# A two-layer mixture-of-experts kernel on one core: tokens of a sample group split one slot sooner, and a shorter, earlier table of groups

## What is computed

```python
gate_scores = softmax(gate_logits)                  # one row of 4 experts per sample
topk_w, topk_i = top_k(gate_scores, 2)              # normalised to sum 1
for e in range(4):
    h = gelu(x @ ew1[e] + eb1[e])                   # 128 -> 512
    y = h @ ew2[e] + eb2[e]                         # 512 -> 128
    out = out + w_be[:, e][:, None, None] * mask[e][None, :, None] * y
shared = gelu(x @ sw1 + sb1) @ sw2 + sb2            # for all samples
return out + shared
```

## Time and profile before

| | |
|---|---|
| median of 3 runs | 917.26 us (915.57 to 918.11) |
| the profiled execution | 918.68 us, span 916.9 us |
| PE busy | 878.2 us, 96% of the span |
| DVE, ACT, POOL busy | 686.0 us (75%), 576.6 us (63%), 407.9 us (44%) |
| granted TensorE clock, mean | 0.993 of full |
| moved by DMA | 82.96 MB, mean 90 GB/s |

### The profile page before, as it was taken

One profiled execution on the slowest core, in us unless ns is written; L12 is line 12 of the kernel. 1 busy time (PEld: TensorE's weight loads), 2 busy tenths in 40 slices (PEclk: granted clock), 3 DMA queues, 4 the chain that ended last, 5 costly groups with the idle time before them and its releaser, 6 DMA issues.

```text
span 916.9 us, 12687 instructions
## 1 busy us (share of the span) xinstructions
PE 878.2 (96%) x3878; PEld 695.8 (76%) x3878; DVE 686.0 (75%) x1098; ACT 576.6 (63%) x1032; POOL 407.9 (44%) x378
## 2 busy tenths in 40 slices
PE   8798788999999999999999999999999998999996
PEld 5587676887888888888888888888888775777773
DVE  7666666787878777677677677676676886998887
ACT  7586667766555455555555555555555667989895
POOL 7436755313535544334244343243322225764465
PEclk9799999999999999999999999999999999999999
DMA  9388876012211410210111111011010059191830
GB/s 313 136 241 263 269 236 193 27 45 81 89 46 46 142 46 1 80 47 6 75 46 35 47 47 69 12 46 47 1 46 1 0 81 182 36 187 48 164 104 35
DMA packets 35828, 82.96 MB, mean 90 GB/s; under 512 B 4400, under 2 KB 14256, under 8 KB 33840
## 3 DMA queue, kind: packets, MB, share of 16 engines
q1 hardware_dynamic: 35760, 82.15, 30.9%
HBM read 71.13 MB, written 6.83 MB: 85 GB/s over the span
## 4 chain that ended last, share of the span: by engine, by line
PE 74%; DVE 8%; issue 5%; ACT 4%; POOL 4%; DMA 3%; POOLq 1%; SPq 1%; DVEq 0%; ACTq 0%
PE ps L882 16%; PE ps L863 16%; PE ps L868 15%; PE ps L917 7%; PE ps L919 7%; PE ps L912 7%; DMA CWB<-scratch 2%; ACT HH L1005 2%; DVE HL L1464 2%; POOL GHL L1539 2%; PE ps L899 1%; PE ps L897 1%; DVE HH L1461 1%; DVE Hf L1451 1%; POOL AC L1554 1%
## 5 line engine op out<-in xcount | busy, mean ns | idle before, releaser
L999 ACT ACTIVATE Sg<-ps 128x512 f32<-128x512 f32 x288 | 171.8, 597 | 246.2 <-PE ps L882 245.7
L1444 DVE TENSOR_TENSOR Hf<-ps,Sg 128x512 f32<-128x512 f32 x288 | 198.0, 688 | 149.3 <-ACT Sg L999 96.2
L1544 POOL TENSOR_TENSOR HL<-Hf,HH 128x512 fp32r<-128x512 f32 x136 | 182.1, 1345 | 172.5 <-ACT HH L1005 155.4
L1005 ACT ACTIVATE HH<-Hf 128x512 fp32r<-128x512 f32 x346 | 216.4, 625 | 24.9 <-DVE Hf L1444 12.8
L1464 DVE TENSOR_TENSOR HL<-Hf,HH 128x512 fp32r<-128x512 f32 x242 | 214.2, 885 | 4.3 <-ACT HH L1005 3.2
L863 PE MATMUL ps<-XHL,WBH 128*128 128x512 f32 x512 | 203.7, 398 | 1.2 <-DVE Hf L1444 1.2
L882 PE MATMUL ps<-XHL,WBH 128*128 128x512 f32 x512 | 202.1, 395 | 0.0
L868 PE MATMUL ps<-XHL,WBL 128*128 128x512 f32 x512 | 202.0, 395 | 0.0
L1559 POOL TENSOR_TENSOR XT<-XT,TMP 128x512 f32<-128x512 f32 x64 | 84.2, 1316 | 251.5 <-DVE TMP L1340 251.5
L863 PEld LDWEIGHTS ps<-XHL,WBH 128*128 128x128 f32 x512 | 96.1, 188 | 25.1 <-DVE Hf L1444 2.3
L1464 DVE TENSOR_TENSOR HL<-ps,HH 128x512 fp32r<-128x512 f32 (+1 forms) x122 | 74.6, 619 | 53.9 <-ACT HH L1005 52.7
(11 more groups left out here) (255 smaller groups left out, 1346.6 us busy)
## 6 DMA issues: line engine op xcount, KB each, us to landing
CWB<-scratch SPq DMA_DIRECT2D x68, 256.0 KB, 8.2
CWB<-scratch SPq DMA_DIRECT2D x15, 1024.0 KB, 4.7
GWD<-expert_down SPq DMA_DIRECT2D x21, 576.5 KB, 4.1
GWU<-expert_up SPq DMA_DIRECT2D x21, 514.0 KB, 4.5
ST<-in_wb_dram SPq DMA_DIRECT2D x8, 768.0 KB, 6.2
GX<-XT SPq DMA_DIRECT2D x68, 64.0 KB, 2.4
XT<-in_x_dram SPq DMA_DIRECT2D x8, 256.0 KB, 5.5
expert_up<-GWU SPq DMA_DIRECT2D x4, 512.0 KB, 3.8
```

The costliest lines, as they stand in the source:

```text
L999: e.activation(Sg[:, it.n % NG, :], zb[z % NZ][:, :], ACT.Silu).then_inc(s_act, 1)
L1005: e.activation(HH[:, it.n % NH, 0:it.cols], hidden_place(it), ACT.Copy).then_inc(s_hi_act, 1)
L1444: e.tensor_tensor(Hf[:, it.n % NS, :], zb[z % NZ][:, :], Sg[:, it.n % NG, :], ALU.mult).then_inc(s_prod, 1)
L1544: e.tensor_tensor(HL[:, it.n % NH, :], Hf[:, it.n % NS, :], HH[:, it.n % NH, :].bitcast(F32), ALU.subtract).then_inc(s_lo_pool, 1)
```

## The change

Three things. (1) `split_g`: the tokens of group g are split in the first slot of group g - 1 instead of its second. (2) The table: `fours` and `twos` are written to PSUM instead of SBUF, the differences `full` and `room` are replaced by one clamped copy `within`, and `low` goes to SBUF. (3) Slots: the sort matmul, the counting and the table matmul one slot sooner, `pairs` directly behind the counting in the same slot (two sooner), `index` and SyncE's first loads one sooner; the expert numbers of the groups (`past`) from slot 17 to 14, the product of `pairs` and weights from 17 to 18; block 5's split on GpSimd from slot 15 to 17.

```diff
-        first_load = 19
-        split_x = {0: (2, 3), 7: (4,), 15: (5,)}
-        g_in, g_best, g_top, g_exp, g_sort, g_key, g_pairs = 9, 10, 11, 12, 13, 14, 15
-        g_table, g_gate, g_index, g_gates, g_weight = 17, 16, 18, 20, 21
+        first_load = 18
+        split_x = {0: (2, 3), 7: (4,), 17: (5,)}
+        g_in, g_best, g_top, g_exp, g_sort, g_key, g_past, g_table = 9, 10, 11, 12, 12, 13, 14, 16
+        g_gate, g_index, g_both, g_gates, g_weight = 16, 17, 18, 20, 21
...
-        split_g = {pos["G", g - 1, 0, 1].k if g else pos["G", 0, 0, 0].k - 1: g for g in range(NGRP)}
+        split_g = {pos["G", g - 1, 0, 0].k if g else pos["G", 0, 0, 0].k - 1: g for g in range(NGRP)}
...
+                fours, twos = bk[0:NB, 64:69], bk[0:NB, 72:77]
                 spare4 = small4[0:NB, 11:16, :].rearrange("p a b -> p (a b)")
-                fours, twos, full, most, room, at4 = [spare4[:, a:b] for a, b in ((0, 5), (5, 10), (10, 14), (14, 18))] + [
-                    u(6), u(7)]
+                within, most, at4, low = spare4[:, 0:5], spare4[:, 5:9], spare4[:, 9:13], spare4[:, 13:17]
...
-                    odd, left, low, at2, end = [v(i) for i in (24, 25, 26, 27, 28)]
+                    odd, left, at2, end = [v(i) for i in (24, 25, 27, 28)]
...
-                    link(e.tensor_tensor(full, fours[:, 1:5], fours[:, 0:4], ALU.subtract))
-                    link(e.tensor_scalar(room, fours[:, 0:4], -1.0, float(FULL), ALU.mult, ALU.add))
+                    link(e.tensor_scalar(within, fours, float(FULL), None, ALU.min))
                     link(e.tensor_scalar(odd, count, 2.0, 3.0, ALU.mult, ALU.add))
                     after()
-                    link(e.scalar_tensor_tensor(out=most, in0=room, scalar=0.0, in1=full, op0=ALU.max, op1=ALU.min))
-                    link(e.scalar_tensor_tensor(out=at4, in0=fours[:, 0:4], scalar=4.0, in1=rank, op0=ALU.mult,
+                    link(e.scalar_tensor_tensor(out=most, in0=fours[:, 1:5], scalar=float(FULL), in1=within[:, 0:4],
+                                                op0=ALU.min, op1=ALU.subtract))
+                    link(e.scalar_tensor_tensor(out=at4, in0=within[:, 0:4], scalar=4.0, in1=rank, op0=ALU.mult,
                                                 op1=ALU.add))
...
-                if k == g_pairs:
                     shape = [NB, 4, NPAIR]
-                    e.wait_ge(f_sm2, 16)
                     after()
                     e.tensor_tensor(pairs[0:NB, 0, :, :], ...
...
-                if k == g_gate + 1:
+                if k == g_both:
                     shape = [NB, 4, NPAIR]
...
-                if k == g_gate + 1:
+                if k == g_past:
                     past = q1[0:1, 0:4 * NGRP].rearrange("p (g e) -> p g e", e=4)
```

## The result

The changed kernel takes 900.76 us (median of 4 runs, 900.39 to 901.11) against 917.37 of the kernel before (4 runs, 915.57 to 918.11): a ratio of 0.9822, 95% interval 0.9805 to 0.9839, 16.6 us. The profiled execution took 900.65 us with a span of 898.9, so span against span it is 18.0 us: the profiled execution of before was 1.3 above the median of its kernel.

What follows compares the result with a forecast made beforehand. TensorE, busy 96%, was taken as the bound, with 17.8 us idle in the group stage and a late table before it. 6.5 + 17.8 - 1.5 - 4.3 - 2.0 = 16.5 us off the median 917.26 gives 900.8, range 894 to 909.

Steps and rivals of the forecast that it cites:

- What bounds the kernel: Whole kernel: TensorE busy 96%, only its gaps can be won; 17.8 us of the group stage idle, nearly all token-split waits.
- Token split one slot sooner: Group stage: GpSimd's split goes ahead of its accumulation's wait for TMP, removing TensorE's waits at L882; 17.8 us gained.
- The table: Before the group stage: table matmul starts at 30.8 instead of 35.59, slot 20 at 38.98 instead of 45.44; 6.5 us gained.
- main case: Whole kernel: all terms of the sum hold, 900.8 us, own range 896 to 906, chance 0.50.
- The rival of a renewed fall: Around the table: clock falls again, 10 us at 1.2 GHz costing 4.5 us, time 903.8; chance 0.13.
- the wait for the product: Slots behind the table: L769 waits 0.5 us for VectorE's product L1170, done at 37.9.
- Group 1's and 2's tokens: Start of group stage: tokens land late for ScalarE's earlier split; TensorE loses 1.2 us, then 0.3; together -1.5.
- SyncE's rounds at the pairs: Group stage, pair groups: SyncE's in-order rounds bring down weights late by 1.3, 1.6, 1.0 and 0.4 us; -4.3, bounds 0 and 4.3.
- T: Group stage: start of pair group 4, from which the walk of SyncE's rounds counts its times.
- Transfers: Group stage: busier DMA engines make down loads land later, half of 0.7 to 1.2 at four borders; -2.0, bounds 0 and 4.8.
- The bound from the DMA share: Group stage: check of the sum; at a share of 0.87 the 87.2 us of transfers need 100.3 us.
- all is recovered: Rival for the whole kernel: SyncE's slack suffices and only the 1.5 are given back, 894.5 us; chance 0.11.

Runs made afterwards that it cites:

- the first experiment: The kernel before with only the new slot of the token split, one slot sooner: 902.89 us, ratio 0.985.
- the table alone: The changed kernel with the token split put back in the second slot of the group before: 914.57 us, ratio 0.9976.
- the last experiment: The changed kernel with an extra 8 KB load per group from the fourth on, three places in turn, each waiting for the one three back: 898.44 us, ratio 0.9795.
- the 8 KB loads that SyncE waits for: The changed kernel with one extra 8 KB load per group from the fourth on, each waiting for the previous extra load: 901.1 us, ratio 0.9821.

## Why the prediction was right, and where only its sum was

Forecast 900.8, measured 900.76. That is closer than its steps were, and that closeness is luck: the stage came out some 3 to 3.5 us better than forecast and the front 1.4 (pair of profiles) to 4 (medians) worse. Where the time goes, and that the token split is the larger part, was right.

- **What bounds the kernel** held. The waits of the earlier trace rows were nearly all of the stage's idle time; they went, and some 5 us of smaller gaps stand in the stage now.
- **Token split one slot sooner, +17.8**: held. GpSimd's order and the idle time that it went into were as stated, and putting back GpSimd's half alone restored every wait.
- **The table, +6.5**: this term was mis-sized. In the pair of profiles the front gave 5.05: table matmul 0.2 late, then 1.2 more, of which 1.0 is the clock below. The path to the table matmul itself was as forecast there (4.58 sooner, 4.8 forecast; 0.51 us from L1118 to L1127, 0.5 forecast). But the profile of before had a slow front: the same code in the first experiment began the stage at 49.19, not 51.12, with held steps of 1.61 instead of 3.04 us and a shorter stretch at the lower clock (mean 0.86 instead of 0.79 from 28 to 52 us). The eight profiles with the changed front and no matmuls added begin it between 45.47 and 48.09, mean 46.7, so between means the gain is (51.12 + 49.19) / 2 - 46.7 = 3.5; by the medians it is 2.1 (the table alone) to 2.9 (16.6 less 13.7). The error is in reading durations of held steps, and of the stretch at the lower clock, from one execution, as if they were the kernel's. How they are spread over many executions of the kernel before is not known; there are two profiles of its front.
- **The clock** fell once, for 3.4 us, where the main case had no fall. The rival of a renewed fall was right in kind (1.6 us of standing still, then small matmuls, was enough in seven of eight profiles) and too dear: I priced 10 us at the lower clock at 4.5; the 3.35 us from 33.61 to 36.96 held 8 matmuls, which take 1.86 at full clock, so it cost 1.5, of which 0.5 was in the forecast already as the wait for the product, which now came in time.
- **Group 1's and 2's tokens, -1.5**: about held in size, not in place. ScalarE waits only 0.19 for group 1's tokens, and TensorE loses nothing at that group's start; it waits 0.55 for those of the next but one, and by the distances between starts TensorE loses 1.2 from 59 to 63 us. In the second profile of the changed kernel it is 0.5. Another 0.4, at the third matmul of the stage, stood in the profile of before too.
- **SyncE's rounds at the pairs, -4.3**: wrong, 0. I gave the border three group lengths of 2.8, 5.6 and 2.8, with each group's own down matmuls in its own slots, but the down matmuls run five slots behind, so a pair's slots still carry those of a four: by the count of their matmuls groups 4, 5 and 6 take 4.2, 4.55 and 3.85 us, and the down weights of group 6 are first read at T + 14.7, not T + 13.3, with the landing forecast at T + 14.5. The trace has more room still: T is 67.16, the three groups take 4.28, 4.65 and 4.38, the load stands at 76.20 (T + 9.0 instead of T + 10.4), and the first matmul on it at 82.66 (T + 15.5).
- **Transfers, -2.0**: 0. The loads did get slower (4.6 and 5.1 us in the median for weights down and up, 4.1 and 4.5 from 50 to 150 us before), but no matmul waited for them. The bound from the DMA share, 100.3 us at 0.87, was near the 101.7 by accident: the share rose to 0.98 in a window where TensorE lacked nothing.
- **Not foreseen, 3.7 us**: 2.4 at the two dense weight splits on GpSimd and 1.3 in seven small gaps near the borders of pairs, most of them behind VectorE's low part. By the distances between starts, 5.3 us of the stage are lost now (0.4, 1.2, 2.4 and 1.3).

The stage was thus forecast at 104.8 and measured at 101.70, 101.03 and 100.97 in the three profiles with the new slot of the split and nothing added, some 3.6 better; the front is worth 3 to 4 less than forecast. Two small slips in the sum do not matter: 13 x 5.57 + 8 x 2.8 is 94.8, not 94.9, and T + 14.5 is 1.2 behind T + 13.3, not 1.3. The stage lies between the main case and the rival "all is recovered", which had it at 97.0 + 1.5 = 98.5; the weight splits (2.4) are most of what is missing to that.

## What to carry to other kernels

Where an in-order engine has a short job that another engine waits for and a long one that waits for somebody else, the short one belongs ahead of the wait, even at no saving of work: 14 of 16.6 us came from one line. Before a gain is read from one profile, look for durations that depend on luck (the 4-element step L1118 took 1.04, 0.94 and 0.15 us in three kernels) and take the low one as the bound of what its removal brings. Count a group's length on the engine that is full with all its work in that window, the lagging half too.

## What the runs showed of the hardware

- The granted clock fell to its lower level (1.2 GHz) for 3.4 us in the changed front after TensorE had stood still for 1.6 us and then done only the small table matmul; of the other profiled kernels with the same wait of 1.6 us, one had no fall (mean clock from 28 to 52 us 1.00, the last experiment) and one had twice as long (0.86, the table alone). With matmuls of 512 columns in the idle time it did not fall in either profiled kernel that had them.
- It also fell inside the stage, for 3.4 us, in the three kernels with GpSimd's split in its old slot and the new slots of the table, where TensorE waited 1.6 to 2.1 us near 100 and 108 us, and with the 8 KB loads that SyncE waits for, behind a wait of 2.0 at 144 us. The length of a wait does not decide it alone: the profile of before has waits of 1.69 and 1.64 us at 105 and 112 us, and its clock stayed at 1.00 through the stage. The row of the table alone:

```profile
105.00:120.00 15.00, 12.54 (x61) 10.38 (x59) 9.19 (x17) 9.32 (x21) 10.20 (x17) 0.89 0.68 207
```

- VectorE steps of 4 elements with all operands in SBUF that started while GpSimd ran a 128x512 instruction ended with that instruction (L1118, L1119 and L1122: 0.38 to 1.28 us). Started between two of GpSimd's instructions, L1118 took 0.15. Not every instruction with all operands in SBUF is held: a TENSOR_REDUCE of the changed kernel (L1177, at 31.81) took 0.23 in the middle of GpSimd's L1490 (31.25 to 32.52).
